# Last expert's tiles put out one place sooner, and GpSimd's loop order changed with it, in a graph network and mixture-of-experts kernel

## The reference

```
shared = gelu(x @ W1s + b1s) @ W2s + b2s
rw     = softmax(x @ Wr);  topw, topi = top_k(rw, 2);  topw /= sum(topw)
h      = gelu(x @ W1p[e] + b1p[e])                 # 256 -> 1024, for 8 experts
priv   = h @ W2p[e] + b2p[e]                       # 1024 -> 256
out    = x + shared + sum over the 2 chosen experts of topw * priv
```

## Time and profile before

| | us |
|---|---|
| median of three runs | 1309.89 |
| lowest and highest of the three | 1306.69, 1316.17 |
| the profiled execution, own time | 1312.32 |
| its span in the trace | 1310.3 |
| TensorE busy | 1198.2 (91% of the span) |
| VectorE busy | 1002.2 (76%) |
| ScalarE busy | 828.7 (63%) |
| GpSimd busy | 772.8 (59%) |
| mean granted TensorE clock | 0.957 of full speed |

### The profile page before, as it was taken

One profiled execution on the slowest core, in us unless ns is written; L12 is line 12 of the kernel. 1 busy time (PEld: TensorE's weight loads), 2 busy tenths in 40 slices (PEclk: granted clock), 3 DMA queues, 4 the chain that ended last, 5 costly groups with the idle time before them and its releaser, 6 DMA issues. The chain is left out here.

```text
span 1310.3 us, 31820 instructions
## 1 busy us (share of the span) xinstructions
PE 1198.2 (91%) x8631; PEld 1107.6 (85%) x8631; DVE 1002.2 (76%) x2523; ACT 828.7 (63%) x2353; POOL 772.8 (59%) x873
## 2 busy tenths in 40 slices
PE   2879999999999999999978889999799999999991
PEld 1669998888888888888867769999799999999991
DVE  7589999999999999999966767544466666665651
ACT  2678888888888888888854565544344444434430
POOL 7167888778887888878852102552245555555552
PEclk9979999999999999999997879999899999999996
DMA  6433333333333333333435462331424434433222
GB/s 239 164 99 99 95 97 97 91 99 96 93 99 95 94 99 95 94 95 96 119 99 178 162 230 91 106 95 51 142 45 109 102 79 110 97 84 74 45 45 25
DMA packets 81050, 135.08 MB, mean 103 GB/s; under 512 B 16190, under 2 KB 56174, under 8 KB 80480
## 3 DMA queue, kind: packets, MB, share of 16 engines
q0 software_dynamic: 31792, 67.29, 21.0%
q1 hardware_dynamic: 45280, 63.66, 14.9%
q10 hardware_dynamic: 3920, 3.41, 0.8%
HBM read 104.73 MB, written 29.57 MB: 102 GB/s over the span
## 5 line engine op out<-in xcount | busy, mean ns | idle before, releaser
L552 POOL DMA_INDIRECT rows<-h_tab,src_st x392 | 402.4, 1027 | 120.0 <-issue 120.0
L576 ACT ACTIVATE hots<-hot,sh_st 128x128 f32<-128x128 f32 x1568 | 467.9, 390 | 2.8 <-PE psY L743 1.7
L743 PEld LDWEIGHTS psY<-prod,hots 128*128 128x128 f32 x2352 | 324.1, 191 | 20.3
L743 PE MATMUL psY<-prod,hots 128*128 128x128 f32 x2352 | 325.6, 275 | 0.0
L740 PE MATMUL psY<-prod,hots 128*128 128x256 f32 x784 | 234.1, 380 | 0.0
L1766 ACT ACTIVATE q_hf<-q_psA,x_b 128x256 f32<-128x256 f32 x232 | 110.0, 474 | 192.0 <-PE q_psA L1311 189.7
L636 DVE TENSOR_TENSOR prod<-psW,rows 128x384 f32<-128x384 f32 x392 | 213.8, 545 | 0.0
L1711 POOL DMA_INDIRECT out_rows<-q_ob,q_index x58 | 119.3, 2057 | 134.8 <-DMA out_rows<-q_ob,q_index 86.3
L1311 PE MATMUL q_psA<-q_xhi,x_whi 128*128 x464 | 133.4, 287 | 7.8 <-DVE q_xlo L1804 7.8
L651 DVE TENSOR_TENSOR y_sb<-y_sb,psY 64x512 f32 x196 | 133.5, 681 | 7.5 <-issue 4.4
L1897 PE MATMUL q_psB<-x_whi,q_hhi 128*128 128x256 f32 x464 | 132.9, 286 | 0.1
(11 more groups left out here) (216 smaller groups left out, 2565.0 us busy)
## 6 DMA issues: line engine op xcount, KB each, us to landing
x_raw<-in_w SPq DMA_DIRECT2D x18, 1024.0 KB, 5.7
cols_lo<-ele_split SPq DMA_DIRECT2D x196, 32.0 KB
rows<-h_tab,src_st POOLq DMA_INDIRECT x392, 2.7
x_sb<-in_x SPq DMA_DIRECT2D x5, 640.0 KB, 5.7
h_tab<-x_sb ACTq DMA_DIRECT2D x5, 640.0 KB, 3.3
u_x<-in_x SPq DMA_DIRECT2D x5, 640.0 KB, 7.2
xnew_d<-u_x SPq DMA_DIRECT2D x5, 640.0 KB, 3.4
xn_d<-u_xn SPq DMA_DIRECT2D x5, 640.0 KB, 4.8
```

Source lines behind the costliest of these rows:

```text
L552: pool.indirect_dma_start(out=rows[p][:, c, :, :].rearrange("p a u -> p (a u)"), out_offset=None, in_=h_tab, in_offset=bass.IndirectOffset ...
L576: ins = nc.scalar.activation(hots[p][:, 4 * c + k, :], hot[p][:, c, :], ACT.Copy, scale=sh_st[p][:, 4 * c + k:4 * c + k + 1])
L743: ins = nc.tensor.matmul(y[:, 2 * k::6 - 2 * k, :][:, 0:2, :], hots[p][:, 4 * c + k + 1, :], a[:, 0::k + 1, :][:, 0:2, :], start=False, st ...
```

## The change

In the last expert each output is moved ahead by one tile on VectorE. Tile 25 is put out at the end of DVE's tile 26 (`late`, f = 7), tile 26 in its tile 27 after `low(s, 1)` (`early`, f = 1), tile 27 in its tile 28 at the same place; tile 28 remains after all tiles. Tiles 23 and 24 keep their places. On GpSimd, in the loop and so for all experts, `landed(d - 1, 1)` goes ahead of `rows_of(d + 4)`. No instruction is added or taken away.

```diff
             with pool.Fori(1, all_but_two) as d:
+                landed(d - 1, 1)
                 rows_of(within(d + 4, TILES + 1))
-                landed(d - 1, 1)
                 add(d, 0)
                 landed(d, 0)
                 add(d, 1)
...
-            def tile(s, e, done=None, after=None):
+            def tile(s, e, done=None, after=None, early=None, late=None):
...
                     if f == 0 and done is not None:
                         output(*done)
+                    if f == 1 and early is not None:
+                        output(*early)
+                    if f == FC - 1 and late is not None:
+                        output(*late)
...
                 tile(first, e, (first, e - 1) if e > 0 else None, split_w2 if e > 0 else None)
+                last = e == EXPERTS - 1
                 tile(within(first + 1), e, (within(first + 1), e - 1) if e > 0 else None,
-                     split_w1 if e + 1 < EXPERTS else None)
+                     None if last else split_w1, late=(within(first + 2), e) if last else None)
                 dve.sem_inc(begun, 1)
-                further(dve, n, first, lambda s, e=e: tile(s, e, (s, e)))
-            output(first + n, EXPERTS - 1)
+                further(dve, n, first, lambda s, e=e, last=last:
+                        tile(s, e, None if last else (s, e), early=(within(s + 1, TILES), e) if last else None))
             output(first + n + 1, EXPERTS - 1)
```

## The result

| | us |
|---|---|
| changed kernel, median of 4 runs | 1347.1 (1342.84 to 1351.44) |
| kernel before beside it, median of 4 runs | 1313.03 (1306.69 to 1318.09) |
| ratio | 1.0262, 95% interval 1.0200 to 1.0324 |
| profiled execution: own time, span | 1351.44, 1349.6 |

The changed kernel is 2.6% slower. The profiled executions differ by 39.1 us, the spans by 39.3. Cut at the adds, the difference lies here. The first add of a tile is a0, with the tile's number; tile 25 is the first of the last expert.

A forecast was written before the change was run, and what follows sets the result against it. The prediction took GpSimd's cycle of adds with VectorE's output, 12.40 us a tile, as the bound. Loop order 26.4 us plus last expert's outputs 9.5 on 1312.3 gave 1348 us; own range 1336 to 1362, 8 in 10 1334 to 1382.

The forecast's parts named there:

- The ring: GpSimd's loop of adds, landing, copies and gathers: 13.42 us a tile in place of 12.40, 25.5 us over 25 tiles.
- First to second add: GpSimd's loop: time from a tile's first add to its second, put at 4.95 us.
- the estimate: GpSimd's loop: from the second add's landing to the first index copy, 0.5 us, which no profile row showed.
- copy to next first add: GpSimd's loop: from first index copy through the gathers to the next tile's first add, put at 4.25 us.
- rival A: GpSimd's loop: first adds turn slow in VectorE's burst, 14.93 us a tile, 1386 us in all; chance 0.22.
- Tile 1 and the tail: Tile 1's first add comes 0.9 us later; tile 26's first add to the last add stays 28.6 us.
- part 2: Last expert: VectorE's early wait holds lows TensorE needs, tile 26's add stands behind a gather; 9.5 us, bounds 8.0 and 12.2.
- X: Last expert: landing of tile 25's second add, from which VectorE's lows and the copies were timed.
- the clock: Last expert: TensorE returns from idle at 1.2 GHz, adding 1.5 us, bounds 0 and 4.2.
- B: Loop: TensorE's idle of about 1.6 us a tile brings the low clock, 1395 us in all; chance 0.05.
- C: Ring stays at 12.4 us and tile 26 is added one TensorE tile sooner, 1301 us; chance 0.04.
- D: Ring grows by only 0.5 us and the last expert's cost is hidden, about 1325 us or less; chance 0.06.

The follow-up runs named there:

- e10_late_everywhere: Changed kernel, but tiles 27 and 28 put the next tile out at f = 7 of VectorE's tile, not f = 1; ratio to before 1.0122.
- e7_no_last_gather: Changed kernel with iteration 26 of GpSimd's loop written out without the unused gather of tile 30; ratio to before 1.0227.
- e11_splits_late_old: Kernel before, with VectorE's splits of the next weights moved from f = 0 to 3 to f = 4 to 7; ratio 1.0100.
- e2_early_only: Changed kernel with the old GpSimd order for all tiles except tile 26, early outputs of the last expert kept; ratio to before 1.0084.
- e1_loop_only: Kernel before with only GpSimd's loop order changed, landing ahead of the gathers, VectorE's outputs unmoved; ratio 1.0205.
- e3_half_old: Kernel before with VectorE's output in halves, each waiting only for the same half's add of the tile before; ratio 0.9894.
- e5_one_gather_new: Kernel before with the new loop order only, second gather of each tile but tile 0 left out; ratio 1.0037.
- e4_half_new: Kernel before with the new loop order and VectorE's output in halves, last expert's outputs unmoved; ratio 1.0267.

## Why the prediction was right

Forecast 1348 us, measured 1347.1; direction and range hold, and both mechanisms are the ones foretold. That the total agrees to 1 us is luck. The forecast stood on one execution of the kernel before, and the profiled pair differs by 39.1 us, of which 2.5 lie ahead of the routed stage and 36.8 in it, against 35.9 said. The upper bound of the forecast's own range is loose as well: 35 and 12 us on 1312.3 give 1359, not 1362.

**The ring.** Sum 13.42 us a tile, measured 13.36 over 24 tiles. The chain of waits after, for the tile shown above:

```profile
1010.88 3.87 DMA out_rows<-q_ob,q_index
...
1015.75 3.73 DMA out_rows<-q_ob,q_index
```

First to second add 4.87 (said: 4.95), second add to landing 3.73 (3.72), landing at 1019.48 to copy at 1019.80 0.32 (0.5, the estimate), copy to next first add 3.81 (4.25). The last was over-sized: the pair of copies took 0.30 us in place of 0.59, and the add stands 0.30 us behind the gather in place of 0.47; why, no run shows. Sum of this undisturbed tile: 12.73, 0.69 under the forecast. The mean lies 0.63 above it, mostly by what the forecast left to rival A: first adds of 4.84 us, 8.22 to the second (1038.21 to 1046.43), and of 3.17 us, and a few slow landings. Median ring 13.0, mean 13.36. Two errors cancelled.

The means over the 24 tiles show what the new order also gave back:

| us a tile | before | after | said |
|---|---|---|---|
| first add to second add | 5.75 | 5.12 | 4.95 |
| second add to copies | 1.40 | 4.37 | 4.22 |
| copies to next first add | 5.27 | 3.87 | 4.25 |

The first row is 15 us over the 24 tiles, and without it the loop order would have cost an estimated 38 us in place of 22.7. It is rival A the other way round. The kernel before was the one with slow first adds, in 12 of these 24 tiles; the prediction had one such row and feared that the new order would bring more. It took nearly all of them away. The forecast has this gain in it, since it took its 4.95 us from an add that stood directly behind its gathers.

**Tile 1 and the tail.** 0.9 said, 0.8 measured; tail unchanged, 0.3 measured.

**The last expert.** Said: part 2's 9.5 us on top of the ring's 1.02, 10.5 in all. Measured 13.0: 2.0 us of the difference lie behind the landing, and 0.5 in that tile 25 took 11.86 us before and not the mean of 12.40. From the landing at X = 1298.28 (1294.50 and 3.78 us in the chain) the copy was put at X + 10.0 and came at X + 12.0. The mis-sized term is the clock: TensorE's 36 matmuls for f = 2 to 7 started 2.75 us behind X and took 7.2 us (next fence), to X + 10.0. VectorE's last low of the tile ended at X + 5.8 (said: X + 5.6), so that at full clock, with 0.70 us for the last group, the matmuls would have ended at X + 6.5. That is about 3.5 us in place of 1.5, within the bounds of 0 and 4.2. TensorE had idled 11.17 us, and the windows show 0.67 and 0.65. The chain of waits after:

```profile
1294.50 3.78 DMA out_rows<-q_ob,q_index
...
1301.03 7.21 PE q_psB L1902 x36
1308.24 1.42 PE q_psA L1311 x12
```

The mechanism itself, VectorE's wait holding the lows and the add behind `rows_of(30)`, is shown by e10_late_everywhere and e7_no_last_gather, each of which removes one half of it. That tile 26's `late` place costs nothing is supported by e10_late_everywhere, which puts all outputs there.

**Rivals.** A came true in part: two of the first adds of tiles 1 to 25 took over 3 us, and ahead of the one of 4.84 us the second gather took 2.51 us in place of 1.00. The Trainium skill (GPSIMD Engine Reference, section 8, Key points) names VectorE's instructions with two SBUF inputs as those that collide with GpSimd. e11_splits_late_old agrees for the weight splits; the lows have two inputs as well, and adds beside them took 1.63 us, so the kind of instruction alone does not tell which add turns slow.

B: most windows of the loop kept 1.00, though TensorE idled up to 1.5 us in a tile; four between 1030 and 1070 us, around the one add of 4.84 us, stood at 0.72 to 0.96, and one at 1210 us at 0.83, without a loss that could be told apart. The lowest of them came behind idles of 1.49 and 2.34 us:

```profile
1050.00:1060.00 10.00, 6.17 (x33) 5.77 (x32) 8.56 (x25) 1.31 (x3) 4.80 (x6) 0.72 0.39 95
```

The fall in every tile that the Trainium skill tells of (TensorE: Matmul & The Clock Gate, section HAM oscillation) did not occur here. C and D are refuted by e2_early_only and e1_loop_only.

**Not tried.** The changed kernel's early outputs with the old loop order for tile 26 too. By the code each would wait for the next in a circle: VectorE in tile 27 for tile 25's landing, which GpSimd would signal only behind the gather of tile 30; that gather for TensorE's `turn(29)` in tile 28; TensorE for VectorE's lows of tile 27. So the early outputs need the new order in that one iteration, which e2_early_only gives them; the other 25 iterations pay for it without need. That the kernel would stop is argued, not run.

## What to carry to other kernels

Where an engine issues DMAs and also waits for them, its order decides what is paid: issue whatever does not need the landing ahead of the wait. A wait on a shared in-order engine is priced by what is queued behind it, and an early result is worth nothing if its consumer stands behind something else. If one buffer of a pair is free, wait for that half alone, and measure it in the order in which it will run: the same edit took 8 us off the 24 tiles in the old order and added 23 in the new one.

## What the runs showed of the hardware

- The same indirect add of 128 rows took 1.55 to 5.4 us on GpSimd. In the kernel before, 12 first adds of 3.2 us ran beside weight splits (two inputs from SBUF); with the splits elsewhere none did, and second adds of up to 4.1 us appeared. But five first adds of e3_half_old that began as close behind a split took 1.64 to 1.78 us, and nine second adds of e5_one_gather_new took 3.2 or 3.3 us with no weight split beside them. In e4_half_new VectorE's burst starts sooner against the landing, with half an output ahead of it, and most first adds took 5.8 to 7.5 us to their successors, against 4.9 in e1_loop_only; that the shift is the cause was argued, not shown.
- Copies and gathers on GpSimd, issued in sequence, left 0.30 us between two gathers and 0.86 to 0.88 us between the index copy and the first gather, in the kernels before and after and in e3_half_old and e7_no_last_gather.
- After 11.17 us of idle TensorE took 7.21 us for 36 matmuls, six groups that take 0.70 us each at 1.00, its granted clock being 0.65 in that window. The first 28 started about 0.21 us apart, the last 8 about 0.12.
